# One pass over sixteen chunks, or over ten groups of one or two chunks

## The chip, the core and the metric

The kernel runs on one core of a Trainium2 chip. Its five engines work at the same time, each through its own list of instructions in order: TensorE (PE in the rows; its weight loads are PEld), VectorE (DVE), ScalarE (ACT), GpSimd (POOL) and SyncE (SP), which issues most of the DMA transfers. They wait for one another through semaphores. The metric is the device time of one execution in microseconds; three executions were timed, and the median counts.

## What is computed

One layer on 2048 tokens of width 128, all in float32: retention attention (linear attention with a decay for each of 8 heads), a residual and a layer norm, then a gated feed-forward part of width 352 whose inputs and weights are rounded blockwise (16 values share a scale) to a four-bit grid, and again a residual and a layer norm.

```python
q, k = rope(x @ Wq), rope(x @ Wk)          # 8 heads of 16
v, g = x @ Wv, x @ Wg                      # 8 heads of 32, width 256
scores = einsum('bhqd,bhkd,hqk->bhqk', q * DQK ** (-0.5), k, decay)   # decay is 0 above the diagonal
o = einsum('bhqk,bhkd->bhqd', scores, v)
o = o * rsqrt(mean(o * o, axis=-1) + EPS) * g_norm_w
x = layernorm(x + (o * silu(g)) @ Wo)
# quant(a): per 16 values, scale = max|a| / 6, each value to the nearest of 0, .5, 1, 1.5, 2, 3, 4, 6 times the scale
h = silu(quant(x) @ quant(w_gate).T) * (quant(x) @ quant(w_up).T)
x = layernorm(x + quant(h) @ quant(w_down).T)
```

## The kernel before

The 2048 tokens are cut into 16 **chunks** of 128 rows, one row to a partition. Attention inside a chunk is a 128 by 128 score tile for each head; what comes from earlier chunks is carried in a small state `S`, updated once for each chunk. So chunks depend on one another through the state alone, and a chunk goes through some forty steps ("stages") on four engines:

- TensorE: `project_qk` and `project_vg`; `transpose_qk`; `scores` (four matmuls, a pair of heads each); `state_product`; `from_state` and `values`, which add into one output; `transpose_o`; `transpose_y`; `out_projection`; then for the feed-forward part `transpose_xq`, `gate`, `up`, `transpose_h`, `down`.
- ScalarE empties most of the results out of PSUM (`copy_scores` into `raw`, `copy_oT`, `squares`, `copy_hT`, `silu_of_gate` and others), does one step of each rounding (`magic_x`, `magic_h`) and the scaling of both layer norms (`ln1_norm`, `ln2_norm`).
- VectorE rotates (`rotate`, three instructions), masks one pair of heads, updates the state, takes the mean square (`mean_square`, tile `ms`), multiplies by the gate (`gated`), adds the residuals, takes the layer norms' statistics and does five of the six steps of each rounding on `x` (128 wide) and on `h` (352 wide).
- GpSimd adds the rotated halves (`rotate_add`), masks the other three pairs of heads (`mask_scores`, `raw` to `probs`), takes the powers to minus one half (`rms_rstd` on 8 values a row, `ln1_rstd`, `ln2_rstd`), multiplies (`gated_output`, tile `y`) and scales back the rounded values (`x_value`, `h_value`).

Each engine's list is written out by the same loop over steps `s`, in which `run(stage, ahead)` issues the stage for chunk `s + ahead`, if there is such a chunk:

```python
for s in range(FIRST, LAST):
    run = stage_runner(s)
    run(state_product, 0)
    run(values, 0)
    run(transpose_xq, -4)
```

So the lines' order and the numbers beside them are the schedule, and nothing else orders the work but semaphores. On TensorE `transpose_xq`, `gate` and `up` are 4 chunks behind `values`, `transpose_h` 7 and `down` 8; on ScalarE the last step, `ln2_norm`, is another 5 behind. Results of TensorE lie in eight PSUM banks of 512 values a row, which several stages share; before a stage writes, it waits until the last tile of that bank was read (`free_scores_bank` and its like). Most tiles in SBUF have two or three buffers, taken by `c % 2` or `c % D`. The four weights are rounded and transposed once, in the gaps of the first steps. SyncE loads `x`, its transpose and the rotation tables in four parts of 1, 2, 5 and 8 chunks, and stores each chunk when it is done.

## Time and profile before

| | |
|---|---|
| timed, median of 3 (lowest to highest) | 140.3 us (139.18 to 141.06) |
| the profiled execution | 140.22 us, of which its trace spans 137.5 us |
| busy: TensorE, VectorE, GpSimd, ScalarE | 121.0, 115.8, 102.9, 97.3 us |
| granted TensorE clock | 0.999 of full speed |
| read and written in HBM | 5.26 MB and 1.05 MB |

The profiled execution lies 0.1 us below the median of the timed ones, and 2.7 us of it lie outside the span. "Busy" counts the time in which an instruction of the engine is under way; instructions of one engine overlap at their ends, so the distance from start to start of two neighbours is shorter than the first one's length where nothing holds the second up. A row of a time view gives start, length, engine, line of the kernel and instruction, and in brackets how long the engine was idle before it and who ended that.

### The profile page before, as it was taken

The numbers are of one execution on the slowest core, as the hardware profiler recorded it, in microseconds if no ns is written. First come the engines' busy times: TensorE is split into PE (matmuls) and PEld (weight loads), VectorE is DVE, ScalarE is ACT, GpSimd is POOL, SyncE is SP. The second block draws the span as 40 slices with busy tenths as digits, with TensorE's granted clock in tenths as the row PEclk, the third lists the DMA queues.
The fourth block names the chain that finished last, engine by engine and source line by source line (L and its number), as shares of the span: only waits on it lengthen the run. The fifth ranks groups of instructions, "written<-read, shape, count | busy, mean of one in ns | idle before, by whom it ended". The sixth has DMA issues, their size and how long they took to land.

```text
span 137.5 us, 3532 instructions
## 1 busy us (share of the span) xinstructions
PE 121.0 (88%) x1224; PEld 77.9 (57%) x1224; DVE 115.8 (84%) x438; ACT 97.3 (71%) x279; POOL 102.9 (75%) x139
## 2 busy tenths in 40 slices
PE   4986897998999999999999999999999878778650
PEld 4833354465656657585858585857575654445440
DVE  1269876867789999999999999999999899999940
ACT  3063965769787887988888888888888666665562
POOL 4204869577797979988888888889899985955692
PEclk9999999999999999999999999999999999999999
DMA  3899980000000000000000000000000000000113
GB/s 112 253 255 232 415 262 7 2 5 2 0 5 0 0 7 0 0 7 0 0 0 5 0 2 5 0 2 5 0 0 24 0 19 19 19 21 19 38 51 104
DMA packets 6897, 6.53 MB, mean 47 GB/s; under 512 B 864, under 2 KB 6112, under 8 KB 6752
## 3 DMA queue, kind: packets, MB, share of 16 engines
q1 hardware_dynamic: 5856, 5.56, 13.5%
q10 hardware_dynamic: 1024, 0.76, 1.7%
q8 instruction: 9, 0.15, 0.4%
q14 instruction: 8, 0.07, 0.2%
HBM read 5.26 MB, written 1.05 MB: 46 GB/s over the span
## 4 chain that ended last, share of the span: by engine, by line
PE 65%; ACT 12%; DVE 8%; DMA 5%; POOL 4%; issue 3%; SPq 1%; POOLq 0%; DVEq 0%; ACTq 0%
PE ps L464 7%; PE ps L480 7%; PE ps L352 6%; PE ps L392 5%; PE ps L335 4%; PE ps L382 4%; PE ps L326 4%; PE ps L457 3%; PE ps L471 3%; PE ps L416 3%; ACT q_eo L511 3%; PE ps L417 3%; DMA wd_nat<-in_w_down 3%; PE ps L365 3%; PE ps L449 3%
## 5 line engine op out<-in xcount | busy, mean ns | idle before, releaser
L899 POOL TENSOR_TENSOR rstd_h<-ms,minus_half 128x8 f32<-128x8 f32 x16 | 26.3, 1644 | 7.9 <-DVE ms L753 7.3
L910 POOL TENSOR_TENSOR rstd<-veps,minus_half 128x1 f32<-128x1 f32 x32 | 18.2, 571 | 1.4 <-DVE veps L769 1.2
L894 POOL TENSOR_SCALAR_AFFINE_SELECT probs<-raw 128x768 f32<-128x768 f32 x16 | 13.8, 863 | 6.9 <-ACT raw L510 6.4
L890 POOL TENSOR_TENSOR qk<-rope_c,rope_s 128x256 f32<-128x256 f32 x16 | 12.2, 766 | 8.2 <-DVE rope_s L730 7.8
L923 POOL TENSOR_TENSOR hq<-h_grid,hs 128x352 f32<-128x352 f32 x16 | 15.0, 935 | 2.9 <-DVE h_grid L667 2.9
L335 PE MATMUL ps<-w_vg,xT_sb 128*128 128x512 f32 x32 | 16.9, 610 | 0.1
L480 PE MATMUL ps<-wd_T,hT 128*128 128x128 f32 x96 | 13.6, 278 | 2.7 <-ACT hT L510 2.7
L464 PE MATMUL ps<-wgu_T,xqT 128*128 128x352 f32 x32 | 13.7, 510 | 1.1 <-DVE r L784 1.1
L480 PEld LDWEIGHTS ps<-wd_T,hT 128*128 128x128 f32 x96 | 12.1, 193 | 3.5 <-DVE r L784 2.6
L510 ACT ACTIVATE raw<-ps 128x768 f32<-128x768 f32 x16 | 13.0, 811 | 0.8 <-PE ps L352 0.6
L510 ACT ACTIVATE hT<-ps 128x384 f32<-128x384 f32 x16 | 7.8, 491 | 7.6 <-PE ps L471 7.6
L511 ACT ACTIVATE q_eo<-ps,consts 128x128 f32<-128x128 f32 x32 | 9.9, 365 | 4.2 <-PE ps L344 4.2
L352 PEld LDWEIGHTS ps<-q_eo,kT 32*128 32x128 f32 x128 | 5.0, 183 | 13.7 <-ACT kT L511 13.7
L352 PE MATMUL ps<-q_eo,kT 32*128 32x256 f32 x128 | 11.4, 426 | 0.9 <-ACT kT L511 0.6
L457 PE MATMUL ps<-wgu_T,xqT 128*128 128x352 f32 x32 | 12.2, 464 | 0.0
L904 POOL TENSOR_TENSOR y<-gate_o,rstd_h 128x256 f32<-128x256 f32 x16 | 10.8, 674 | 1.3
L726 DVE TENSOR_TENSOR rope_c<-ps,tabs_sb 128x256 f32<-128x256 f32 x16 | 6.6, 414 | 5.7 <-PE ps L326 5.5
L510 ACT ACTIVATE oT<-ps 128x256 f32<-128x256 f32 x16 | 6.1, 383 | 7.1 <-PE ps L392 7.1
L392 PE MATMUL ps<-probs,v_sb 128*32 128x128 f32 x256 | 10.6, 274 | 0.2 <-POOL probs L894 0.2
L574 ACT ACTIVATE o_sq<-ps 128x256 f32<-128x256 f32 x16 | 6.1, 384 | 6.5 <-PE ps L401 6.5
L806 DVE TENSOR_TENSOR h_blocks<-ps,silu_h 128x352 f32<-128x352 f32 x16 | 8.3, 522 | 2.5 <-PE ps L464 2.4
L326 PE MATMUL ps<-w_qk,xT_sb 128*128 128x256 f32 x32 | 10.4, 409 | 0.0
(108 smaller groups left out, 353.6 us busy)
## 6 DMA issues: line engine op xcount, KB each, us to landing
tabs_sb<-rope_tables SPq DMA_DIRECT2D x1, 1024.0 KB, 11.2
out<-x SPq DMA_DIRECT2D x16, 64.0 KB, 1.5
tabs_sb<-rope_tables SPq DMA_DIRECT2D x1, 640.0 KB, 7.8
xT_sb<-x_transposed SPq DMA_DIRECT2D x1, 512.0 KB, 9.1
x_res<-x SPq DMA_DIRECT2D x1, 512.0 KB, 11.8
xT_sb<-x_transposed SPq DMA_DIRECT2D x1, 320.0 KB, 6.6
x_res<-x SPq DMA_DIRECT2D x1, 320.0 KB, 8.3
w_vg<-in_w_vg ACTq DMA_DIRECT2D x1, 256.0 KB, 3.4
```

Source lines behind the costliest of these rows:

```text
L326: mm(qk_ps, xT(c), w_qk[:], start=True, stop=True).then_inc(qk_pe, 1)
L335: mm(vg_ps, xT(c), w_vg[:], start=True, stop=True).then_inc(vg_pe, 1)
L352: last = mm(sc_ps(j), kT[rows, c % D, :], q_eo[rows, c % D, :, :].rearrange("p e q -> p (e q)"), start=True, stop=True)
L392: last = mm(oT_ps[32 * slot32:32 * slot32 + 32, n // 4, :], v_sb[:, c % D, n * DV:(n + 1) * DV], probs[:, c % 2, n, :], start=c == 0, stop ...
L457: mm(gate_ps, xqT[:, c % 2, :], wgu_T[:, 0:I], start=True, stop=True).then_inc(gate_pe, 1)
L464: mm(up_ps, xqT[:, c % 2, :], wgu_T[:, I:2 * I], start=True, stop=True).then_inc(up_pe, 1)
L480: last = mm(down_ps, hT[:, c % 2, t, :], wd_T[:, t, :], start=t == 0, stop=t == 2)
L510: copy = lambda o, i: nc.scalar.activation(o, i, ACT.Copy)
L511: scaled = lambda o, i, by: nc.scalar.activation(o, i, ACT.Identity, scale=by)
L899: gp.tensor_tensor(rstd_h[:, c, :], ms[:, c, :], minus_half[:], ALU.pow).then_inc(rms_p, 1)
L910: gp.tensor_tensor(rstd[n][:, c, :], veps[n][:, c, :], minus_half[:, 0:1], ALU.pow).then_inc(ln_p[n], 1)
L923: gp.tensor_tensor(hq[:, c % 2, 0:I].rearrange("p (n k) -> p n k", k=BLK), h_grid[:, c % 2, :].rearrange("p (n k) -> p n k", k=BLK), hs[:, ...
```

## The change

The 16 chunks are put into ten **groups**: one chunk, six times two, three times one. The loop of each engine now runs over groups. Three kinds of stages are told apart: `run` calls a stage once for a group, `run_first` and `run_second` for its first and its second chunk.

A stage of a whole group is one instruction on VectorE, ScalarE or GpSimd, on twice the data where the group is a pair; on TensorE it is as many matmuls as before, behind one wait and with one signal at their end. Single by chunk are: `project_vg`, `from_state`, `gate`, `up`, `transpose_h` and the evacuations behind them (a bank holds one chunk of these), `next_state`, `h_product`, and what takes a scale or bias for each row and chunk (`ln1_centre`, `ln1_norm`, `ln2_norm`, the statistics of the layer norms). The widths of a pair's instructions: 512 for the rotation, gate and mask tiles of 256, 1536 for the scores' copy and mask, 256 for `x`, 704 for `h`, 16 and 2 values for the powers.

With it go: other places in PSUM (`QK`, `YT` and `ATT` share bank 4, `QKT` lies in bank 0 with scores, the two chunks' `oT` take banks 0 and 1, 2 and 3); two buffers for a group's tiles, by `g % 2`, and one only of `raw` and `probs`; a state for each chunk; the first and second layer norm and the output share one tile `r`; the tables in HBM are laid out by group; the loads have 1, 2, 4 and 9 chunks; the output is stored by group, in 10 transfers instead of 16. The lines of all four loops stand in another order, with other numbers beside them: on TensorE `transpose_xq` and the first `gate` are 3 groups behind `values`, `transpose_h` 6 and `down` 7, on ScalarE `ln2_norm` is 5 to 6 behind that. TensorE and the other engines compute the same results; the matmuls' number and shapes are the same.

```diff
--- before.py
+++ after.py
 MB = 1
 EPS = 1e-5
 
+SIZES = [1, 2, 2, 2, 2, 2, 2, 1, 1, 1]
+NG = len(SIZES)
+FIRSTS = [sum(SIZES[:g]) for g in range(NG)]
+
...
-        sc_ps = lambda j: ps[:, j, 0:256]
-        oT_ps = ps[:, 0:2, 0:C]
-        o_ps = ps[:, 2, 0:VD]
-        yT_ps = ps[:, 3, 0:VD]
-        qk_ps = ps[:, 4, 0:256]
-        qkT_ps = ps[:, 4, 256:512]
-        vg_ps = ps[:, 5, :]
-        att_ps = ps[:, 5, 0:H]
-        gate_ps = ps[:, 6, 0:I]
-        xqT_ps = ps[:, 6, 384:512]
-        hT_ps = ps[:, 6, 0:384]
-        up_ps = ps[:, 7, 0:I]
-        down_ps = ps[:, 7, 384:512]
-        U_ps = ps[:, 7, 0:2 * DV]
+        QK, QKT, VG, STATE, O, YT, ATT, XQT, GATE, UP, HT, DOWN = 4, 0, 5, 7, 2, 4, 4, 6, 6, 7, 6, 7
+        oT_ps = lambda i, half: ps[:, 2 * i + half, 0:C]
+        gate_ps = ps[:, GATE, 0:I]
+        up_ps = ps[:, UP, 0:I]
+        hT_ps = ps[:, HT, 0:384]
...
-        GROUPS = ((0, 1), (1, 3), (3, 8), (8, NC))
-        group = lambda c: next(g for g, (a, b) in enumerate(GROUPS) if a <= c < b)
-
-        FIRST, LAST = -4, 29
+        ends = [FIRSTS[1], next(f for f in FIRSTS if f >= 3), next(f for f in FIRSTS if f >= 7), NC]
+        LOADS = list(zip([0] + ends, ends))
+        load_of = lambda c: next(k for k, (a, b) in enumerate(LOADS) if a <= c < b)
+
+        first, size = FIRSTS.__getitem__, SIZES.__getitem__
+        last_of = lambda g: first(g) + size(g)
+
+        where = lambda c: (group(c) % 2, c - first(group(c)))
+
+        FIRST, LAST = -26, -1
         def stage_runner(s):
 
+
             def run(stage, ahead):
-                if 0 <= s + ahead < NC:
+                if 0 <= s + ahead < NG:
                     stage(s + ahead)
-            return run
+
+            def run_first(stage, ahead):
+                if 0 <= s + ahead < NG:
+                    stage(first(s + ahead))
+
+            def run_second(stage, ahead):
+                if 0 <= s + ahead < NG and size(s + ahead) == 2:
+                    stage(first(s + ahead) + 1)
+            return run, run_first, run_second
...
-            for c in range(NC):
-                sp.wait_ge(x2_act, c + 1)
-                sp.dma_start(out[c * C:(c + 1) * C, :], x2[:, c, :]).then_inc(d_out, 16)
-            sp.wait_ge(d_out, 16 * NC)
+            for g in range(NG):
+                sp.wait_ge(x2_act, last_of(g))
+                sp.dma_start(out[first(g) * C:last_of(g) * C, :].rearrange("(c p) n -> p c n", p=C),
+                             r[:, first(g):last_of(g), :]).then_inc(d_out, 16)
+            sp.wait_ge(d_out, 16 * NG)
...
-            def project_qk(c):
+            def project_qk(g):
                 pe.wait_ge(d_wqk, 16)
-                pe.wait_ge(d_x[group(c)], 16)
-                free_qk_bank()
-                mm(qk_ps, xT(c), w_qk[:], start=True, stop=True).then_inc(qk_pe, 1)
-                fill(4, "qk")
-                if c == 0:
+                pe.wait_ge(d_x[load_of(first(g))], 16)
+                free(QK)
+                for i in range(size(g)):
+                    last = mm(ps[:, QK, i * 256:(i + 1) * 256], xT(first(g) + i), w_qk[:], start=True, stop=True)
+                last.then_inc(qk_pe, 1)
+                fill(QK, "qk")
...
+            def scores(g):
+                pe.wait_ge(qkT_act, 3 * (g + 1))
                 for j in range(NP):
-                    free_scores_bank(j)
-                    rows = slice(32 * j, 32 * j + 32)
-                    last = mm(sc_ps(j), kT[rows, c % D, :], q_eo[rows, c % D, :, :].rearrange("p e q -> p (e q)"),
-                              start=True, stop=True)
+                    free(j)
                     tile[j] = "sc"
+                for i in range(size(g)):
+                    for j in range(NP):
+                        rows = slice(32 * j, 32 * j + 32)
+                        last = mm(ps[:, j, i * 256:(i + 1) * 256], kT[rows, g % 2, i, :],
+                                  q_eo[rows, g % 2, i, :, :].rearrange("p e q -> p (e q)"), start=True, stop=True)
                 last.then_inc(sc_pe, 1)
                 filled["sc"] += 1
...
-            def state_product(c):
-                if c == NC - 1:
+            def state_product(g):
+                chunks = [c for c in range(first(g), last_of(g)) if c < NC - 1]
-                free_up_bank()
-                pe.wait_ge(qk_p, c + 1)
-                pe.wait_ge(vg_act, c + 1)
-                for j in range(NP):
-                    last = mm(U_ps[32 * j:32 * j + 32, :], qk[:, c % D, 128 + 32 * j:160 + 32 * j],
-                              v_sb[:, c % D, 64 * j:64 * j + 64], start=True, stop=True)
+                free(STATE)
+                pe.wait_ge(qk_p, g + 1)
+                pe.wait_ge(vg_act, chunks[-1] + 1)
+                for i in range(len(chunks)):
+                    for j in range(NP):
+                        last = mm(ps[32 * j:32 * j + 32, STATE, i * 2 * DV:(i + 1) * 2 * DV],
+                                  qk[:, g % 2, i, 128 + 32 * j:160 + 32 * j], v_sb[:, g % 2, i, 64 * j:64 * j + 64],
+                                  start=True, stop=True)
                 last.then_inc(U_pe, 1)
-                fill(7, "U")
+                tile[STATE] = "U"
+                filled["U"] += len(chunks)
...
             def from_state(c):
-                pe.wait_ge(qkT_act, 3 * (c + 1))
+                g, i = group(c), c - first(group(c))
+                pe.wait_ge(qkT_act, 3 * (g + 1))
                 pe.wait_ge(state_v, c)
-                free_scores_bank(0)
-                free_scores_bank(1)
-                tile[0] = tile[1] = "oT"
-                filled["oT"] += 1
+                for half in range(2):
+                    free(2 * i + half)
+                    tile[2 * i + half] = "oT"
+                if i == 0:
+                    filled["oT"] += 1
                 if c == 0:
                     return
...
-            def down(c):
+                fill(HT, "hT")
+
+            def down(g):
                 pe.wait_ge(wT_act, 3)
-                free_up_bank()
-                pe.wait_ge(hT_act, c + 1)
-                for t in range(3):
-                    last = mm(down_ps, hT[:, c % 2, t, :], wd_T[:, t, :], start=t == 0, stop=t == 2)
+                free(DOWN)
+                pe.wait_ge(hT_act, last_of(g))
+                for i in range(size(g)):
+                    for t in range(3):
+                        last = mm(ps[:, DOWN, i * H:(i + 1) * H], hT[:, g % 2, i, t, :], wd_T[:, t, :], start=t == 0,
+                                  stop=t == 2)
                 last.then_inc(down_pe, 1)
-                fill(7, "down")
...
-                run = stage_runner(s)
-                run(state_product, 0)
-                run(values, 0)
...
+                run, run_first, run_second = stage_runner(s)
+                run_second(gate, 20)
+                run_second(project_vg, 24)
+                run(scores, 24)
+                run_second(up, 20)
...
-            def copy_scores(c):
-                act.wait_ge(sc_pe, c + 1)
-                copy(raw[:, c % 2, :, :].rearrange("p (j e) q -> p j (e q)", e=2), ps[:, MB:4, 0:256]).then_inc(
-                    raw_act, 1)
-
-            def copy_oT(c):
-                act.wait_ge(o_pe, c + 1)
-                copy(oT[:, c % 2, :, :], oT_ps).then_inc(oT_act, 1)
-
-            def squares(c):
+                copy(v_sb[:, b, i, :], ps[:, VG, 0:VD])
+                nc.scalar.activation(silu_g[:, b, i * VD:(i + 1) * VD], ps[:, VG, VD:2 * VD], ACT.Silu).then_inc(vg_act, 1)
+
+            def copy_scores(g):
+                act.wait_ge(sc_pe, g + 1)
+                k = size(g) * 256
+                copy(raw[:, :, 0:k], ps[:, MB:4, 0:k]).then_inc(raw_act, 1)
...
             def ln2_norm(c):
 
-                act.wait_ge(ln_v[1]["sum"], c + 1)
-                act.wait_ge(ln_p[1], c + 1)
-                scaled(x2[:, c, :], r[1][:, c, :], rstd[1][:, c, :]).then_inc(x2_act, 1)
+                act.wait_ge(ln_v[1]["sum"], group(c) + 1)
+                act.wait_ge(ln_p[1], group(c) + 1)
+                scaled(r[:, c, :], r[:, c, :], rstd[1][:, c, :]).then_inc(x2_act, 1)
...
-            def mask_scores(c):
+                cos, sin = (tabs_sb[:, a + m * n * H:a + (m + 1) * n * H].rearrange("p (g f) -> p g f", f=16)
+                            for m in range(2))
+                src, dst = g16(ps[:, QK, 0:n * 256]), g16(rope_s[:, b, 0:n * 256])
+                vec.tensor_tensor(g16(rope_c[:, b, 0:n * 256]), src, cos.unsqueeze(2).to_broadcast([128, 8 * n, 2, 16]),
+                                  ALU.mult).then_inc(rope_v, 1)
+                vec.scalar_tensor_tensor(dst[:, :, 0, :], src[:, :, 1, :], -1.0, sin, ALU.mult, ALU.mult).then_inc(rope_v, 1)
+                vec.tensor_tensor(dst[:, :, 1, :], src[:, :, 0, :], sin, ALU.mult).then_inc(rope_v, 1)
...
-            def ln_eps(n, c):
-                dve.wait_ge(ln_v[n]["aggr"], c + 1)
-                vec.tensor_scalar(veps[n][:, c, :], mv[n][:, c, 1:2], EPS, None, ALU.add).then_inc(ln_v[n]["eps"], 1)
-
+            def ln_eps(n, g):
+                dve.wait_ge(ln_v[n]["aggr"], last_of(g))
+                chunks = slice(first(g), last_of(g))
+                vec.tensor_scalar(veps[n][:, chunks, 0], mv[n][:, chunks, 1], EPS, None, ALU.add).then_inc(
+                    ln_v[n]["eps"], 1)
+
...
-            def rms_rstd(c):
-                pool.wait_ge(ms_v, c + 1)
-                gp.tensor_tensor(rstd_h[:, c, :], ms[:, c, :], minus_half[:], ALU.pow).then_inc(rms_p, 1)
-
+            def rms_rstd(g):
+                pool.wait_ge(ms_v, g + 1)
+                a, n = first(g), size(g)
+                flat = lambda t: t[:, a:a + n, :].rearrange("p c h -> p (c h)")
+                gp.tensor_tensor(flat(rstd_h), flat(ms), minus_half[:, 0:n * NH], ALU.pow).then_inc(rms_p, 1)
+
```

**TensorE, near the start.** In the rows `qk` and `kT` are the rotated keys and queries, `q_eo` the scaled queries, `oT` the heads' outputs. Before, from the projection of chunk 1 on, which follows the scores of chunk 0:

```order
L326 MATMUL ps<-w_qk,xT_sb 128x256
L365 MATMUL ps<-v_sb,qk 32x64 x4
L392 MATMUL ps<-probs,v_sb 32x128 x8
L400 MATMUL ps<-ident,oT 128x128
L401 MATMUL ps<-ident,oT 128x128
L343 MATMUL ps<-ident,qk 128x128
L344 MATMUL ps<-ident,qk 128x128
L335 MATMUL ps<-w_vg,xT_sb 128x512
L352 MATMUL ps<-q_eo,kT 128x256 x4
L326 MATMUL ps<-w_qk,xT_sb 128x256
```

Now, from the projection of the first pair, chunks 1 and 2, on:

```order
L326 MATMUL ps<-w_qk,xT_sb 128x256 x2
L336 MATMUL ps<-w_vg,xT_sb 128x512
L374 MATMUL ps<-v_sb,qk 32x64 x4
L406 MATMUL ps<-probs,v_sb 32x128 x8
L415 MATMUL ps<-ident,oT 128x128 x2
L348 MATMUL ps<-ident,qk 128x128 x4
L336 MATMUL ps<-w_vg,xT_sb 128x512
L360 MATMUL ps<-q_eo,kT 128x256 x8
L326 MATMUL ps<-w_qk,xT_sb 128x256 x2
L336 MATMUL ps<-w_vg,xT_sb 128x512
```

The transposes and scores of chunks 1 and 2 stand together, and the projection of chunks 3 and 4 right behind them; before, chunk 2's scores stood one whole turn behind chunk 1's.

**TensorE, at the end** (`xq` and `hq` are the rounded inputs, `wgu_T` and `wd_T` the weights, `hT` the transposed hidden values). Before:

```order
L457 MATMUL ps<-wgu_T,xqT 128x352
L464 MATMUL ps<-wgu_T,xqT 128x352
L471 MATMUL ps<-ident,hq 128x128 x3
L480 MATMUL ps<-wd_T,hT 128x128 x3
L471 MATMUL ps<-ident,hq 128x128 x3
L480 MATMUL ps<-wd_T,hT 128x128 x3
L471 MATMUL ps<-ident,hq 128x128 x3
L480 MATMUL ps<-wd_T,hT 128x128 x3
L471 MATMUL ps<-ident,hq 128x128 x3
L480 MATMUL ps<-wd_T,hT 128x128 x3
```

Now:

```order
L496 MATMUL ps<-ident,hq 128x128 x6
L506 MATMUL ps<-wd_T,hT 128x128 x6
L470 MATMUL ps<-ident,xq 128x128
L480 MATMUL ps<-wgu_T,xqT 128x352
L488 MATMUL ps<-wgu_T,xqT 128x352
L496 MATMUL ps<-ident,hq 128x128 x3
L506 MATMUL ps<-wd_T,hT 128x128 x6
L496 MATMUL ps<-ident,hq 128x128 x3
L506 MATMUL ps<-wd_T,hT 128x128 x3
L496 MATMUL ps<-ident,hq 128x128 x3
L506 MATMUL ps<-wd_T,hT 128x128 x6
```

Behind the last `gate` and `up` stood the hidden transposes and `down` of the last chunks in turn, four times; now the transposes of the last three groups (single chunks) stand before the `down` of a pair, of a single chunk, and of the last two single chunks in a row.

**ScalarE, at the end** (`hT` as above; `x` before and `r` now is the output that `ln2_norm` scales). Before:

```order
L510 ACTIVATE hT<-ps 128x384
L528 ACTIVATE h_magic<-h_ratio 128x352
L511 ACTIVATE x<-r,rstd 128x128
L510 ACTIVATE hT<-ps 128x384
L511 ACTIVATE x<-r,rstd 128x128
L510 ACTIVATE hT<-ps 128x384
L511 ACTIVATE x<-r,rstd 128x128 x7
```

Now:

```order
L544 ACTIVATE r<-r,rstd 128x128
L543 ACTIVATE hT<-ps 128x384
L561 ACTIVATE h_magic<-h_ratio 128x352
L544 ACTIVATE r<-r,rstd 128x128
L543 ACTIVATE hT<-ps 128x384
L544 ACTIVATE r<-r,rstd 128x128 x2
L543 ACTIVATE hT<-ps 128x384
L544 ACTIVATE r<-r,rstd 128x128 x12
```

Behind the last copy of `hT` stand 12 output scalings, where 7 stood before.

## Rows read from the trace of the kernel before

**Rows 1.** The page's first lines: span, and busy time, share and instructions of each engine.

```profile
span 137.5 us, 3532 instructions
...
PE 121.0 (88%) x1224; PEld 77.9 (57%) x1224; DVE 115.8 (84%) x438; ACT 97.3 (71%) x279; POOL 102.9 (75%) x139
```

**Rows 2.** Stretches: length; busy (count) of PE, PEld, DVE, ACT, POOL; clock, DMA.

```profile
20.40:38.42 18.02, 16.45 (x201) 9.94 (x198) 13.55 (x47) 13.18 (x39) 13.42 (x17) 1.00 0.02 4
38.42:56.09 17.67, 17.49 (x202) 10.60 (x202) 16.43 (x64) 14.30 (x45) 15.11 (x20) 1.00 0.01 2
60.79:101.34 40.55, 40.55 (x459) 27.20 (x458) 38.73 (x156) 32.73 (x97) 35.14 (x44) 1.00 0.01 2
107.99:137.50 29.51, 18.99 (x104) 12.33 (x103) 24.20 (x97) 17.24 (x48) 19.56 (x29) 1.00 0.12 34
```

**Rows 3.** Chain in order of time: start, length, what; one chunk's turn.

```profile
60.79 0.67 PE ps L480 x6
61.46 0.59 PE ps L457 x2
62.06 0.86 PE ps L335 x2
62.91 0.64 PE ps L352 x8
...
64.35 0.33 PE ps L471 x3
64.68 0.43 PE ps L326 x2
65.33 0.38 PE ps L382 x16
65.96 0.44 PE ps L392 x16
```

**Rows 4.** VectorE in order of time: start, length, instruction.

```profile
69.83 0.52 DVE L658 SCALAR_TENSOR_TENSOR h_ratio<-h_blocks,hs 128x352 f32<-128x352 f32 x1
70.27 0.29 DVE L761 BATCH_NORM_STATS2 stats<-r 128x6 f32<-128x128 f32 x1
70.47 0.41 DVE L736 TENSOR_TENSOR probs<-ps,causal 128x256 f32<-128x256 f32 x1
```

**Rows 5.** GpSimd's groups: busy time, mean ns of one, idle before it.

```profile
L899 POOL TENSOR_TENSOR rstd_h<-ms,minus_half 128x8 f32<-128x8 f32 x16 | 26.3, 1644 | 7.9 <-DVE ms L753 7.3
...
L910 POOL TENSOR_TENSOR rstd<-veps,minus_half 128x1 f32<-128x1 f32 x32 | 18.2, 571 | 1.4 <-DVE veps L769 1.2
...
L923 POOL TENSOR_TENSOR hq<-h_grid,hs 128x352 f32<-128x352 f32 x16 | 15.0, 935 | 2.9 <-DVE h_grid L667 2.9
...
L904 POOL TENSOR_TENSOR y<-gate_o,rstd_h 128x256 f32<-128x256 f32 x16 | 10.8, 674 | 1.3
...
L894 POOL TENSOR_SCALAR_AFFINE_SELECT probs<-raw 128x768 f32<-128x768 f32 x16 | 13.8, 863 | 6.9 <-ACT raw L510 6.4
```

**Rows 6.** GpSimd in order of time, one chunk's loop from mask to mask.

```profile
21.90 0.86 POOL L894 TENSOR_SCALAR_AFFINE_SELECT probs<-raw 128x768 f32<-128x768 f32 x1
...
27.19 0.62 POOL L904 TENSOR_TENSOR y<-gate_o,rstd_h 128x256 f32<-128x256 f32 x1
...
27.76 0.86 POOL L894 TENSOR_SCALAR_AFFINE_SELECT probs<-raw 128x768 f32<-128x768 f32 x1
```

**Rows 7.** Chain in order of time: chunk 1's transposes, chunk 4's scores.

```profile
13.01 0.33 PE ps L343
...
32.45 0.71 PE ps L352 x8
```

**Rows 8.** ScalarE at the end: last hidden copy, three and then the last output.

```profile
131.74 0.49 ACT L510 ACTIVATE hT<-ps 128x384 f32<-128x384 f32 x1 [1.16 <-PE ps L471]
...
132.13 1.01 ACT L511 ACTIVATE x<-r,rstd 128x128 f32<-128x128 f32 x3
...
135.07 0.40 ACT L511 ACTIVATE x<-r,rstd 128x128 f32<-128x128 f32 x1 [0.27 <-POOL rstd L910]
```

767 lines of the change are left out of this document (413 added, 354 removed).

## The prediction

> **What bounds the kernel now.** The page's first lines show TensorE busy 88% and VectorE 84% of the span [rows 1]; the stretches tell where. From 60.79 to 101.34 six chunks pass in 40.55 us, 6.76 us each, TensorE without a break and VectorE at 38.73 of 40.55 [rows 2]: TensorE is the bound, VectorE is just under it. The chain there gives its prices [rows 3]: `down` 0.67, `gate` or `up` 0.59, `project_vg` 0.86, `scores` 0.64, three transposes 0.33 (0.11 each), `project_qk` 0.43, `from_state` 0.38, `values` 0.44. With seven more transposes, `out_projection` at 2 x 0.22 (`down` is three such) and about 0.14 for `state_product` a chunk is 6.28 us of work; 0.48 us are gaps where stages change. Attention is 4.0 of it, `transpose_xq`, `gate` and `up` 1.3, `transpose_h` and `down` 1.0.
>
> Before that, TensorE has less to do and the kernel is no faster for it: 18.02 us for three chunks, then 17.67 us for three [rows 2], 6.0 and 5.9 each. What closes there is a loop through GpSimd: mask, `values`, `copy_oT`, `transpose_o`, `squares`, mean square, power, `y`, and the next chunk's mask, 27.76 - 21.90 = 5.86 us [rows 6], in which the power alone is 1.64 [rows 5]. After 107.99, when the last chunk's mean square starts, 29.5 us remain; VectorE is busy for 24.20 of them, TensorE for 18.99 [rows 2]. So there are three regimes: a latency loop, TensorE, and an end where VectorE's queue and latencies decide.
>
> **What an instruction costs on VectorE.** `h_ratio`, 352 wide, lasts 0.52 us, but its follower starts 0.44 us after it; the 128-wide statistics lets its own follower start after 0.20 [rows 4]. So a value costs 0.24/224 = 1.07 ns and 0.06 to 0.07 us are fixed per instruction from start to start. Of 26 instructions for a chunk, 20 become one for a pair: 10 fewer for each chunk of a pair, 0.65 us of 6.3. With these prices, summed over the whole list in its new order, VectorE goes from 107.8 us to 100.3 (438 instructions [rows 1] to 305). The Trainium skill (VectorE: DVE Perf Modes, section "The TRN2 errata") states a measured fixed term of about 150 cycles for each instruction, exposed between instructions, and advises wide tiles. At 0.157 us each the 133 fewer would save 21 us, not 8; the lengths agree with it (0.52 less 352 values is 0.15), the start distances do not, and I go by these.
>
> **The fill.** Chunk 0 stays alone, so I keep its times, up to the next transposes at 13.0 [rows 7]; with two chunks they end at 13.6. Then, worked from rows and doubled widths: three scaled copies 1.4, scores of both chunks 1.3 (until 16.3), copy of 1536 scores 1.45, mask 1.55 (below 2 x 0.863 [rows 5], above 0.863), `values` 0.9, `out_projection` of chunk 0 0.44, transposes of `oT` and of the next keys 1.3 with waits, until 22.1. With the copies 1.4 more the scores of chunks 3 and 4 start at 23.5. Chunk 4's started at 32.45 [rows 7]: **9 us earlier**, since one passage of the chain now carries two chunks.
>
> For a pair the loop of 5.86 grows by its wider instructions: mask 0.69; the power on 16 values; `y` 0.57; and 1.6 to 1.8 for `values`, `out_projection`, transposes, squares and mean square. The power took 1.644 us on 8 values and 0.571 on one, 0.153 a value, so 2.87 on 16, 1.23 more; the ends are 1.64 (nothing more) and 3.29 (double). The loop is then 9.9 us a pair, 5.0 a chunk in place of 5.9. By it the mean square of group 2 is at 32.0 us, with five chunks done.
>
> **The middle.** Seven turns follow, until the last group's mean square. TensorE's work in each, from the stages that its list holds there: 10.7 (8.0 attention, 1.4 weights, 1.3 the first feed-forward chunk), 9.4, 10.6, 10.3, 8.6, 8.6, 6.9. VectorE's, by its list: 5.4, 7.3, 9.5, 9.7, 9.8, 9.2, 8.2. Stages change about as often in a turn of two chunks as in one before, so I add 0.5 to TensorE's; where VectorE is longer I add 0.3, its loss in a 6.76 us turn being 0.3. The longer of the two: 11.2, 9.9, 11.1, 10.8, 10.1, 9.5, 8.5, sum 71.1. The last mean square starts at 32.0 + 71.1 = 103.1 us, 4.9 earlier than 107.99. So of 9 us gained in the fill 4 are given back: the feed-forward part now runs 3 to 7 groups behind, up to 12 chunks where it was 8, so that attention is nearly over before the first `down`, and three turns of one chunk are bound by VectorE with a pair's rounding in them. Shorter gaps alone would give 0.24 a chunk; that is in the sum.
>
> **The end.** From the last mean square to the last `h_grid` VectorE's list has 21.1 us. I add 1.5 for waits: at 125.7 us. `h_value` 0.94 [rows 5], transposes 0.33, `copy_hT` 0.49 and three handovers: 2.2, so 127.9. From the last mean square to the end of that copy it was 24.2 before (107.99 to 131.74 + 0.49 [rows 8]), now 24.8. Behind the copy the last chunk's `down`, residual, statistics, power and scaling take until 135.07 + 0.40, 3.2 us. Now ScalarE has 12 scalings queued there instead of 7, 0.30 us from start to start ((1.01 - 0.40)/2 [rows 8]), 3.7 us: a new wait, 0.5 longer than the chain it covers. Ends 131.6, and 2.0 for the last transfer as before (137.5 - 135.47): span 133.6, and with 2.7 outside it **136.3 us**. The profiled execution, 140.22, stands 0.1 below the median, so this is also the median's forecast: 3% faster.
>
> At no price I set: the merged loads and stores (transfers are idle, 0.02 and less, in the first three stretches [rows 2]); the new sharing of banks 4 and 0, since `rotate` (1.3 us) and the copies end before the next writer is due, 1.5 us or more of TensorE's work later; one buffer for `raw` and `probs`, whose next writer needs `values` anyway. If that cover fails a turn grows by some 0.3.
>
> **Rivals.** (1) *The pair's loop does not open.* With the feed-forward part in the list TensorE needs 10.3 to 10.6 for a turn, and by the same prices the mask ends only 0.4 us before `values` wants it. VectorE's long rounding instructions (704 values, 0.80 us) stand ahead of `mean_square`, GpSimd's `h_value` of 704 (1.7 to 1.9) ahead of the power, and `ln1_norm`, which waits for a power behind the next mask, stands ahead of `copy_oT`. If these put 1.2 us into each of six turns, the kernel takes 136.3 + 7.2 = 143.5 us, slower. From 0.7 us a turn it is slower than before, from 1.1 by over 2%. Against it: each such delay has some slack in the list, and the power may be cheaper than linear. GpSimd's rows also say that VectorE slows it: `y` has a mean of 0.674 [rows 5], against 0.62 where VectorE has much less to do [rows 6]. The Trainium skill (SBUF — State Buffer, section "SBUF: two separate sides") says that a VectorE instruction with two SBUF inputs and a GpSimd one lock each other out for a whole instruction, and these get longer here: by that 0.8 us at a time, which is this rival; the rows show stretches of 0.1 us.
>
> (2) *TensorE alone bounds the middle, and the end is as lean as before.* If VectorE's fixed cost that goes is nearer to the 0.15 us of its durations than to 0.07, it drops below TensorE in every turn: 65.1 + 7 x 0.5 = 68.6 in place of 71.1. With the power at some 2.2 in the fill and at the end (1.2 less) and 1.2 less of VectorE's list behind the last mean square, 131.4 us. This is also what the skill's fixed term above would make of the time.
>
> (3) *The gain of the fill is spent at the end.* The last groups are single, and each waits for VectorE, GpSimd, TensorE and ScalarE in turn, with little else queued; before, ScalarE stood 1.16 before the last copy of `hT` alone [rows 8]. With 5 us of waits in place of 1.5 it is 139.8: no change. That the change doesn't merge what it says is excluded by the list.
>
> **Chances and range.** The forecast's case 0.42 (133.5 to 139), the fast one 0.28 (129 to 133.5), the spent gain 0.14 (138.5 to 141), the closed loop 0.16 (140 to 147). The power's bounds are worth -1.5 and +2 us, the gaps' (0.2 to 1.0 a turn) -2 and +3.5. From 130.5 to 142 some eight in ten are held. A measurement of this kernel tells some 2% from no change, 2.8 us: faster than 137.5 has 0.28, and 0.29 of the 0.42; same (137.5 to 143.1) 0.28; slower 0.15, rounded.
>
> **What would show it.** Right: scores 8 matmuls at a time, the second such block at about 23.5 us; the power on 16 values near 2.87; the last mean square near 103; TensorE at 0.9 and more from 32 to 84 us and under it after; VectorE over 0.95 from 74 to 115; ScalarE with a dozen scalings without a break at the end. Wrong: TensorE waiting in each turn before `values` or `transpose_y` for GpSimd (rival 1), a last mean square before 100 (rival 2), or VectorE idle for more than 3 us after 105 (rival 3). The weakest steps are the 0.5 for gaps, and that a turn costs the larger of two sums although each engine waits for the other inside it.

## The result and the profile after

The changed kernel takes 141.09 us (median of 20 executions, 140.41 to 141.90), the one before 139.94 (20 executions beside them, 139.04 to 142.23): **1.0091 times the time, 95% interval 1.0062 to 1.0120**. It is 0.9% slower, where 3% faster was forecast. The ratios leave out executions over 1.5% slower than the fastest of the same kernel. The profiled execution has a span of 139.2 us and a time of 141.9, so it is the slowest of the 20, 0.8 us above the median.

The page of the changed kernel begins so (busy time and share of the span by engine; TensorE's clock in 40 slices, in tenths of full speed):

```profile
span 139.2 us, 3261 instructions
PE 120.4 (87%) x1224; PEld 80.2 (58%) x1224; DVE 110.4 (79%) x317; ACT 90.6 (65%) x219; POOL 94.3 (68%) x91
PEclk9999999999999999999999999999999999999868
```

Against [rows 1] VectorE has 121 instructions fewer (the prediction counted 133) and is busy 5.4 us less, but TensorE's work is the same. The mean squares mark the groups, which are counted from 0 (VectorE in order of time, groups 2, 3 and 9):

```profile
32.31 0.70 DVE L810 TENSOR_REDUCE ms<-o_sq 128x16 f32<-128x528 f32 x1
44.07 0.70 DVE L810 TENSOR_REDUCE ms<-o_sq 128x16 f32<-128x528 f32 x1
...
106.64 0.43 DVE L810 TENSOR_REDUCE ms<-o_sq 128x8 f32<-128x264 f32 x1
```

Below, "interval" is the time between the mean squares of two groups, and "end" the time from the last one to the end of the span. Three stretches of the same kernel (from 32.31, group 2's mean square; busy time of PE, PEld, DVE, ACT, POOL; clock, DMA) show where each engine is the bound, to be read against [rows 2]:

```profile
32.31:77.47 45.16, 44.12 (x542) 29.00 (x540) 34.99 (x95) 34.70 (x81) 34.94 (x26) 1.00 0.01 1
77.47:106.64 29.17, 27.66 (x257) 17.95 (x256) 28.99 (x80) 21.35 (x57) 23.77 (x20) 1.00 0.01 3
106.64:139.20 32.56, 21.67 (x120) 15.41 (x118) 24.93 (x90) 16.70 (x45) 17.68 (x22) 0.93 0.12 32
```

First TensorE is full (all but 1.04 us) and VectorE idles for 10 us. Then VectorE is full. The end is 3.1 us longer than the 29.5 of [rows 2]. So VectorE has idle time in the first stretch, where TensorE is the bound, and almost none in the second, where it is the bound itself.

The fill came as forecast: the scores of chunks 3 and 4 start at 24.08 where [rows 7] have chunk 4's at 32.45, and the power on 16 values takes 2.91 us.

```profile
24.08 1.15 PE L360 MATMUL ps<-q_eo,kT 32*128 32x256 f32 x16 [0.82 <-DVE gate_o L816]
```

But it isn't work done earlier. By 34 us TensorE has been busy for 28.3 us in the kernel before and for 28.6 us in the changed one:

```profile
0.00:34.00 34.00, 28.29 (x273) 17.28 (x274) 22.68 (x73) 19.86 (x52) 19.21 (x30) 1.00 0.51 156
```

```profile
0.00:34.00 34.00, 28.62 (x320) 18.73 (x320) 23.22 (x58) 19.51 (x44) 18.79 (x24) 1.00 0.50 156
```

The scores of chunk 4 are 8.4 us earlier, and the feed-forward part, which the old order did in that time, is later.

### The profile page after: what moved, and what is told of

It reads as the page before. It is cut to its first block, busy times and chain, and to the rows that moved or that the text cites. A ratio compares the mean times of both kernels' runs of the same rounds, so it can differ in the third digit from the quotient of the medians.

```text
span 139.2 us, 3261 instructions
## 1 busy us (share of the span) xinstructions
PE 120.4 (87%) x1224; PEld 80.2 (58%) x1224; DVE 110.4 (79%) x317; ACT 90.6 (65%) x219; POOL 94.3 (68%) x91
## 3 DMA queue, kind: packets, MB, share of 16 engines
HBM read 5.26 MB, written 1.05 MB: 45 GB/s over the span
## 4 chain that ended last, share of the span: by engine, by line
PE 50%; DVE 33%; ACT 6%; issue 4%; POOL 3%; POOLq 0%; DVEq 0%; ACTq 0%
PE ps L336 7%; PE ps L360 5%; PE ps L326 5%; PE ps L506 4%; DVE h_ratio L710 4%; PE ps L406 4%; PE ps L480 4%; PE ps L488 3%; DVE h_plus L715 3%; DVE hs L702 3%; PE ps L395 3%; DVE h_grid L719 3%; PE ps L435 3%; DVE h_blocks L876 3%; PE ps L319 2%
## 5 line engine op out<-in xcount | busy, mean ns | idle before, releaser
L983 POOL TENSOR_TENSOR rstd_h<-ms,minus_half 128x16 f32<-128x16 f32 (+1 forms) x10 | 24.0, 2404 | 13.9 <-DVE ms L810 13.9
L996 POOL TENSOR_TENSOR rstd<-veps,minus_half 128x2 f32<-128x2 f32 (+1 forms) x20 | 14.1, 711 | 10.0 <-DVE veps L829 9.9
L1013 POOL TENSOR_TENSOR hq<-h_grid,hs 128x704 f32<-128x704 f32 (+1 forms) x10 | 14.7, 1468 | 4.2 <-DVE h_grid L719 4.2
L974 POOL TENSOR_SCALAR_AFFINE_SELECT probs<-raw 128x1536 f32<-128x1536 f32 (+1 forms) x10 | 13.2, 1316 | 4.5 <-ACT raw L543 4.4
L968 POOL TENSOR_TENSOR qk<-rope_c,rope_s 128x512 f32<-128x512 f32 (+1 forms) x10 | 12.8, 1282 | 4.3 <-DVE rope_s L783 4.3
L506 PE MATMUL ps<-wd_T,hT 128*128 128x128 f32 x96 | 13.8, 295 | 0.5 <-DVE r L848 0.4
L543 ACT ACTIVATE raw<-ps 128x1536 f32<-128x1536 f32 (+1 forms) x10 | 11.9, 1194 | 3.5 <-PE ps L360 3.5
L496 PE MATMUL ps<-ident,hq 128*128 128x128 f32 x48 | 8.5, 288 | 3.9 <-POOL hq L1013 2.0
L990 POOL TENSOR_TENSOR y<-gate_o,rstd_h 128x512 f32<-128x512 f32 (+1 forms) x10 | 9.8, 975 | 0.8
L561 ACT ACTIVATE h_magic<-h_ratio 128x704 bf16<-128x704 f32 (+1 forms) x12 | 8.0, 665 | 3.1 <-DVE h_ratio L710 3.1
L715 DVE SCALAR_TENSOR_TENSOR h_plus<-h_magic,h_ratio 128x704 f32<-128x704 bf16 (+1 forms) x12 | 9.7, 818 | 0.0
## 6 DMA issues: line engine op xcount, KB each, us to landing
tabs_sb<-rope_tables SPq DMA_DIRECT2D x1, 1152.0 KB, 10.3
```

The lines of the kernel that those rows point to most:

```text
L496: last = transpose(hT_ps[:, t * C:(t + 1) * C], hq[:, b, i, t * 128:(t + 1) * 128], ident[:])
L506: last = mm(ps[:, DOWN, i * H:(i + 1) * H], hT[:, g % 2, i, t, :], wd_T[:, t, :], start=t == 0, stop=t == 2)
L543: copy = lambda o, i: nc.scalar.activation(o, i, ACT.Copy)
L715: vec.scalar_tensor_tensor(plus, magic, MAGIC, ratio, ALU.max, ALU.add).then_inc(count["plus"], 1)
L974: gp.affine_select(out=probs[:, MB:, 0:n, :, :].rearrange("p j i e q -> p j (i e) q"), in_=raw[:, :, 0:n * 256].rearrange("p j (k q) -> p ...
L983: gp.tensor_tensor(flat(rstd_h), flat(ms), minus_half[:, 0:n * NH], ALU.pow).then_inc(rms_p, 1)
```

## The experiments

Ratios are to the kernel before, with the 95% interval; the changed kernel itself has 1.0091. The table has, for each kernel, the intervals from group 2's mean square on and the end, worked out from the starts of the mean squares in each trace (us). TensorE's granted clock from 131 to 136 us stands beside the five kernels whose ends are compared by it. The intervals can be compared to 0.1 us, the spans can't: the first mean square starts anywhere from 13.8 to 15.6 us in these profiled executions.

```
forecast                 11.2 9.9 11.1 10.8 10.1 9.5 8.5  end 30.5
changed kernel           11.8 10.2 11.6 11.6 10.3 10.1 8.8  end 32.6  clock 0.66
e1_bank7                 10.7 10.2 11.6 11.6 10.3 10.1 8.8  end 31.5  clock 1.00
e2_down_first            11.7 10.2 11.6 11.6 10.3 10.1 8.8  end 31.7  clock 0.85
e3_fill_matmuls          11.8 10.2 11.6 11.6 10.3 10.1 8.8  end 32.8  clock 1.00
e4_ratio_first           11.8 10.2 12.0 11.5 10.5 10.3 8.8  end 33.6  clock 0.66
n0_state_early           10.4 10.2 12.0 11.9 10.3 10.1 8.8  end 31.5
t1_no_state_read         10.3 10.3 11.3 11.2 10.2 10.1 8.6  end 31.1
t5_no_power              10.6  9.9 11.6 11.6 11.1 10.3 9.0  end 31.0
t6_no_power_no_state     10.3 10.1 11.3 11.2 11.1 10.3 8.8  end 31.8
t2_half_rounding         10.6 10.2 11.6 11.3  9.7  9.7 8.4  end 29.4
t3_rotate_on_vector      11.0 11.0 11.9 11.3 10.2 10.1 8.8  end 31.5
```

**e1_bank7**, one wait:

```
-                    pe.wait_ge(wT_act, 2 if filled["weights"] == 1 else 3)
+                    pe.wait_ge(wT_act, 2 if bank == UP or filled["weights"] == 1 else 3)
```

> The changed kernel (1.009 times the time of the kernel before) with one wait shortened: the first state product of the pair in turn 3 waited 1.04 us for the copy of the down weights (bank 6), though its own bank 7 needs only the copy of the gate and up weights. Theory A (this wait is on the path of the middle turns): turn 3 shrinks by 0.6 to 1.0 us, the last mean square starts at 105.6 to 106.0 instead of 106.64, ratio 1.002 to 1.005. Theory B (the turn is set by another chain, GpSimd's or VectorE's): nothing moves, 1.007 to 1.011.

Measured: **1.0007, 0.9976 to 1.0039**. Group 3's mean square came 11.76 us after group 2's in the changed kernel and 10.65 here, so the wait of 1.04 us counted in full. This is TensorE's row of the changed kernel there (start, length, what, the idle time before it and who ended it):

```profile
39.37 0.43 PE L374 MATMUL ps<-v_sb,qk 128*32 128x64 f32 x16 [1.04 <-ACT wd_T L543]
```

TensorE idles for 1.04 us while ScalarE is still to copy another bank's weights: theory A, at a ratio just below its range (the last mean square starts at 106.39, later than it said, because the whole fill of that execution starts 0.8 us later). The two ratios differ by 1.2 us, each known to 0.4 us. So this wait is as much as the changed kernel lost against the one before, within what can be measured. One thing isn't separated from it: the granted clock, as a mean over an execution, was 0.982 to 0.993 in the 20 executions of the changed kernel and 0.991 to 0.996 in the 11 compared here. The following kernels, but for e2 to e4 and m1, have the edit too, and are compared with 1.0007.

**e2_down_first**, TensorE's order from the group's turn -10 on, with the old call kept for the turns ahead of that:

```
+                if s >= -10:
+                    run(down, 17)
                 run_first(transpose_h, 18)
```

> The changed kernel with the down products of a group ahead of the hidden transposes of the next group in TensorE's order, for the last groups only. Theory A (the end is 2 us longer than forecast because down of group 8 stands behind transposes that wait for the last hq, and down of group 9 then waits for the residual of group 8): the span from the last mean square to the end is 1 to 2 us shorter than 32.6, ratio 0.996 to 1.002. Theory B (the end is set by the last hq and the products' length at the lower clock): under 0.4 us, 1.006 to 1.010.

**e3_fill_matmuls**, up to 7 at the end of a turn, 3 ahead of the last transposes:

```
+            def filler(n):
+                free(3)
+                for _ in range(n):
+                    mm(ps[:, 3, 0:C], ident[:], ident[:], start=True, stop=True)
```

> The changed kernel with extra 128-wide matmuls into a bank that nothing reads, in TensorE's idle time of the last six turns (results unchanged). Theory A (TensorE's granted clock falls in the last 14 us because it idles, and the last down products last 1.29 and 1.53 us instead of 0.67 and 0.91 for that): clock over 0.9 there, last products 0.7 to 0.9, 0.7 to 1.2 us less, ratio 1.001 to 1.005. Theory B (the clock falls anyway, or the extra matmuls delay others by as much): 1.008 to 1.015.

Measured: e2 1.0096 (1.0055 to 1.0137), e3 1.0142 (1.0091 to 1.0193), theory B's ranges for both. The order of the products is worth nothing in the time, though e2's profiled end is 0.8 us shorter than the changed kernel's, at a higher clock. In e3 the clock stayed at 1.00 and the last two `down` took 0.83 and 0.94 us, its last mean square was no earlier against the first, and its end was 0.2 longer: the extra matmuls cost what they bring. That TensorE's clock is lower at the end of some executions is seen in the chain's last `down` products, of the changed kernel first, then of e1_bank7:

```profile
131.70 1.29 PE ps L506 x6
133.36 1.53 PE ps L506 x6
```

```profile
131.27 0.68 PE ps L506 x6
132.32 0.95 PE ps L506 x6
```

1.2 us between the two pairs, and the ends differ by 1.1. Both programs have the same instructions there; what differs is the wait some 90 us before, and whether it has to do with the clock at the end isn't shown. The changed kernel's 20 times don't follow its mean clock: the two executions at 0.988 took 140.4 us, the two at 0.993 took 141.6.

**e4_ratio_first**: `run(h_ratio_, 20)` moved ahead of `run(h_grid_, 19)` in VectorE's order.

> The changed kernel with VectorE's h_ratio (704 values) ahead of h_grid of the group before, so that it runs at another time than GpSimd's addition of the rotated parts, beside which it lasted 1.41 instead of 0.88 us in three turns. Theory A (such meetings stretch instructions and the turns with them): h_ratio near 0.88 in all turns, the turns 7 to 9 shorter by 0.3 to 0.5 each, ratio 0.999 to 1.005. Theory B (a meeting only moves to the next wide instruction, h_grid, 0.82 alone, and GpSimd waits as before): h_grid 1.2 to 1.4, turns unchanged, 1.007 to 1.012.

Measured: 1.0213 (1.0167 to 1.0259). Theory B, and worse than its range: the intervals together are 0.7 us longer than the changed kernel's and the end 1.0. VectorE's rows of the changed kernel, then of this one:

```profile
84.35 0.83 DVE L719 SCALAR_TENSOR_TENSOR h_grid<-h_magic,h_plus 128x704 f32<-128x704 bf16 x1
85.09 1.41 DVE L710 SCALAR_TENSOR_TENSOR h_ratio<-h_blocks,hs 128x704 f32<-128x704 f32 x1
```

```profile
85.26 0.89 DVE L710 SCALAR_TENSOR_TENSOR h_ratio<-h_blocks,hs 128x704 f32<-128x704 f32 x1
86.07 1.42 DVE L719 SCALAR_TENSOR_TENSOR h_grid<-h_magic,h_plus 128x704 f32<-128x704 bf16 x1
```

The stretch (0.53 us there, 0.6 here) stays and hits whichever comes second, beside GpSimd's addition; `h_grid`, for which GpSimd waits, now starts 7.8 us after the mean square instead of 6.9 and lasts longer.

**The sizes of the groups.** With e1's edit, `SIZES` is [1]*16; [1, 2, 2, 2] + [1]*9; and [1, 2, 2, 2, 2, 2] + [1]*5, with more turns in the loop.

> The changed kernel with the shortened wait of bank 7 (e1_bank7, 1.0007), and sixteen groups of one chunk: the new order of stages and no merged instruction. Theory A (merging is worth nothing by itself in the middle, since TensorE takes as long for a pair as for two, and its gain in the fill is spent by the longer distance to the feed-forward part): 0.99 to 1.01. Theory B (merging saves VectorE's fixed 0.06 to 0.15 us in some 130 instructions and GpSimd's, and most of that counts): 1.03 to 1.07.

> As h1_all_single, in groups of one, three pairs, nine single ones: pairs only where the latency loop of the fill decides. Theory A (pairs gain in the fill, and the lag of the feed-forward part that they make, counted in groups, costs at the end): better than e1_bank7, 0.97 to 0.99. Theory B (the end doesn't depend on the groups' size, VectorE's total does): worse than e1_bank7, 1.01 to 1.03.

> As h1_all_single, in groups of one, five pairs, five single ones. Theory A: between h2_three_pairs and e1_bank7, 0.985 to 1.000. Theory B: 1.002 to 1.012, between e1_bank7 and the kernel with more single groups.

Measured: 1.1557 (1.1496 to 1.1618), 1.0939 (1.0841 to 1.1038), 1.0353 (1.0290 to 1.0417). Theory A fails on all three, and theory B, right in sign, put the loss at less than half: in the new order merging is worth 22 us (162.10 against 140.05). The chain of h1 over one turn of one chunk (start, length, what) shows why:

```profile
82.89 0.28 ACT oT L543
...
83.21 0.44 PE ps L415 x2
83.65 0.61 PE ps L480 x2
...
84.28 0.46 ACT silu_h L632
84.74 0.26 ACT q_eo L544
...
85.57 0.71 PE ps L360 x8
...
88.83 0.28 DVE S L805
...
89.70 0.98 POOL rstd L996
...
90.76 0.40 ACT x_blocks L544
91.16 0.28 ACT oT L543
```

It comes back to its start after 8.27 us: `copy_oT`, transposes, SiLU and the scaled queries, scores, TensorE's list up to the state product, VectorE's first state update, `amax` of `h` (tile `hs`) and `eps`, GpSimd's power for the first normalisation, and `ln1_norm`, which stands ahead of `copy_oT` on ScalarE. The order before took 6.76 us a chunk [rows 2]. So the new order alone loses, and merging wins that back: two chunks in 10.2 to 11.6 us.

Now the other way: later pairs need the second state update ahead of the residual on VectorE.

```
                 run_first(next_state, 24)
+                run_second(next_state, 24)
```

> e1_bank7 (1.0007, 11.6 us in turns 4 and 5, span end 31.5 behind the last mean square) with VectorE's second state update of a pair right behind the first, which frees bank 7 earlier; it is also what later pairs need. Theory A (TensorE's own work bounds the middle): no change, 0.998 to 1.003. Theory B (the order on VectorE holds TensorE back there): 0.5 to 2 us less, 0.985 to 0.997.

> As n0_state_early, in nine groups: one, seven pairs, one. h3_five_pairs (eleven groups) was 1.0353, e1_bank7 (ten) 1.0007. Theory A (a turn costs what the pair's rounding in it costs, also where its attention is for one chunk, so that each group fewer saves): 3 to 5 us less than n0, 0.965 to 0.98. Theory B (pairs at the end lengthen the last chain, each of its steps having two chunks, by as much as a turn saves): 0.995 to 1.02.

> As n1_pairs_to_end, in eight pairs, also the first and the last. Theory A: one turn less again, but the first chain has two chunks, some 0.6 to 2 us: 0.95 to 0.98. Theory B (the first chain and the last chain with pairs cost more than a turn): worse than n1, 1.00 to 1.03.

Measured: n0 1.0075 (1.0034 to 1.0116), n1 1.0152 (1.0107 to 1.0197), n2 1.0325 (1.0267 to 1.0383). n0 costs 1 us, where 0 or a gain was expected: the two intervals of 11.6 are 0.35 and 0.32 us longer, and an earlier one 0.2 shorter. It is the loop of h1. VectorE's second state update, some 0.3 us, now stands ahead of `eps`. So GpSimd idles for 1.16 us before the first normalisation's power, where it was 0.84 in e1_bank7, and TensorE idles before the transposes behind `copy_oT`, where it never did in those two turns:

```profile
74.62 0.70 POOL L996 TENSOR_TENSOR rstd<-veps,minus_half 128x2 f32<-128x2 f32 x1 [1.16 <-DVE veps L829]
76.36 0.66 PE L415 MATMUL ps<-ident,oT 128*128 128x128 f32 x4 [0.20 <-ACT oT L543]
```

n1 saves a turn, its last mean square being 7.0 us earlier than n0's, at 100.5, and its end is 40.0 instead of 31.5: theory B. So is n2, a little above its range. Ten groups are the best of the six splits, of which the last two also have n0's edit.

**What a turn hangs on.** From e1_bank7, the products with the state left out; GpSimd's power on the mean squares made a multiplication; both; and, in VectorE's two last rounding steps, half of the values:

```
-                if c == 0:
+                if c >= 0:
                     return
```

```
-                gp.tensor_tensor(flat(rstd_h), flat(ms), minus_half[:, 0:n * NH], ALU.pow).then_inc(rms_p, 1)
+                gp.tensor_tensor(flat(rstd_h), flat(ms), minus_half[:, 0:n * NH], ALU.mult).then_inc(rms_p, 1)
```

```
+            h_half = lambda buf, g: buf[:, g % 2, 0:size(g) * I // 2]
```

> e1_bank7 with TensorE's products of the queries with the state left out, 0.76 us of each pair's turn (the output lacks the part that comes from earlier chunks). Theory A (TensorE bounds turns 4 and 5, VectorE turns 7 to 9): the intervals between mean squares from group 4 to 6 shrink from 11.6 to 10.9, those from group 7 on don't, the last mean square starts 1.5 to 2.5 us earlier. Theory B (a loop through all engines bounds every turn alike): all intervals shrink by the same 0.3 to 0.8, or none does.

> e1_bank7 with GpSimd's power on the mean squares (2.91 us for a pair) replaced by a multiplication (so the normalisation of the heads is wrong): the loop mask, values, squares, power, y is 2.7 us shorter. Theory A (in the fill and up to turn 4 the loop decides, from turn 5 TensorE's work and the loop end about together): the intervals from group 0 on, 8.8, 9.6, 10.7, 10.2, lose 1.5 to 2.7 each until TensorE's work of 10 to 11 stops it; those of 11.6 lose 0.2 at most; 10.3, 10.1, 8.8 nothing. Theory B (the loop decides in no turn after the fill): only the first two shrink.

> Both left out, the power and the products with the state (0.76 us of TensorE's work in a turn). Theory A (TensorE's work and the loop end together in turns 5 and 6, which is why t1 alone gave 0.3 to 0.4 of its 0.76): the intervals of 11.6 become 10.9. Theory B (TensorE alone, its durations overlapping): 11.2 as in t1_no_state_read. Turns 7 to 9 unchanged in both.

> e1_bank7 with VectorE's h_plus and h_grid on half of their values (the other half of the hidden values isn't rounded), 2 x 0.37 us less in the turn of a pair, 2 x 0.18 in that of one chunk. Theory A (VectorE bounds turns 7 to 9 and the end): the intervals 10.3, 10.1, 8.8 lose 0.7 to 0.8 each, the end 1.0 to 1.8 us, the earlier ones nothing. Theory B (the late turns hang on waits between engines): 0.2 to 0.4 each and under 0.8 in the end.

Measured once each: 137.82, 140.63, 138.38 and 137.19 us. t5 is the surprise: 2.7 us less in what the prediction took for the loop, and the first intervals go from 8.8 and 9.6 to 8.8 and 9.4, no other shrinks by more than 0.3, and one, in which VectorE is busy throughout, grows by 0.8. Neither theory. In t1 0.4 of the 0.76 come back in each of the two turns of 11.6, half of what theory A wanted, and in t6 the same: with the power gone too nothing more is gained. TensorE is no longer full there. It idles for 0.23 and 0.26 us in the two turns, in both kernels. In the first it waits for VectorE's rotation; what it waits for in the second a row of t1 shows:

```profile
74.17 0.66 PE L415 MATMUL ps<-ident,oT 128*128 128x128 f32 x4 [0.26 <-ACT oT L543]
```

It is the loop of h1, and ScalarE waits in it also in the changed kernel:

```profile
63.26 0.40 ACT L544 ACTIVATE x_blocks<-r_mean,rstd 128x128 f32<-128x128 f32 x1 [1.00 <-POOL rstd L996]
```

That loop holds one of the two `from_state` of a pair, 0.38 us, and so loses as much in t1. With n0, where the loop grows by 0.3 us and the turns by as much, this says that in these turns TensorE's work and the loop take the same time, to 0.1 us or so. Rival 1 feared this for another loop. t2 bears theory A out for the end (2.1 us less, from 2.6 less of VectorE's work) and half for the late turns (10.3, 10.1 and 8.8 become 9.7, 9.7 and 8.4, 1.4 us for 2.7 less of VectorE's work): VectorE is the bound there, and TensorE, busy in t2 for 27.1 of these 27.8 us, close behind.

**t3_rotate_on_vector**: GpSimd's `rotate_add` goes to the end of VectorE's `rotate`.

> e1_bank7 with the addition of the rotated parts on VectorE (some 0.6 us more of its work in a turn of a pair) instead of GpSimd (0.96 to 1.9 us less of its). Theory A (meetings with GpSimd cost VectorE about what they last, 0.5 us at h_ratio and 0.4 at x_grid in turns 7 to 9): h_ratio 0.88 there, VectorE's turns as long as before, and the fill 0.5 a turn shorter: 0.99 to 1.00. Theory B (each microsecond added to VectorE counts, since the meetings cost it nothing net): turns 7 to 9 0.5 longer, 1.008 to 1.02.

Measured: 1.0223 (1.0172 to 1.0274). The fill loses, intervals 8.8 and 9.6 becoming 9.5 and 10.8, as VectorE has the additions for pairs in it (1.13 and 1.80 us long there). The late turns don't: with 0.53 us more in VectorE's list they stay at 10.2, 10.1 and 8.8, and `h_ratio` is back at 0.88:

```profile
84.87 0.53 DVE L786 TENSOR_TENSOR qk<-rope_c,rope_s 128x256 f32<-128x256 f32 x1
87.55 0.88 DVE L710 SCALAR_TENSOR_TENSOR h_ratio<-h_blocks,hs 128x704 f32<-128x704 f32 x1
```

Theory A for the late turns (an addition on GpSimd costs VectorE what doing it itself would), B's sign in the total, just above its range.

**m1_port**, the price by itself.

> A kernel that leaves the layer out and writes zeros: VectorE and GpSimd instructions of this kernel's shapes alone and then side by side. Theory A (an exclusive lock between a VectorE instruction with two SBUF inputs and a GpSimd one): h_ratio's form of 704 values 0.88 alone and up to 1.4 to 1.8 beside GpSimd's additions of 512, the 352-wide one 0.52 and up to 1.0 to 1.4; the form with a PSUM input, and that with one input, unchanged; the additions 0.96 alone and longer in the first case only; the sum of both engines' work in the shared stretch about the sum of their lone times. Theory B (shared bandwidth): all forms stretched alike, in proportion to their length, about 1.3 to 1.6 times.

Its rows: busy time of VectorE and GpSimd in stretches where VectorE runs six of a form alone (`h_ratio`'s with 704 and 352 values, one with a PSUM input, one with a single SBUF input), then the first two beside GpSimd's additions of 512, `h_ratio`'s of 704 beside its power on 16, and the last two beside additions.

```profile
6.00:10.90 4.90, 4.89 (x6) 0.00 (x0) 1.00 0.00 0
10.90:13.67 2.77, 2.71 (x7) 0.00 (x0) 1.00 0.00 0
...
18.60:22.30 3.70, 3.68 (x6) 0.00 (x0) 1.00 0.00 0
22.30:25.10 2.80, 2.70 (x6) 0.00 (x0) 1.00 0.00 0
...
47.00:65.80 18.80, 18.80 (x11) 18.71 (x10) 1.00 0.00 0
67.40:82.20 14.80, 14.76 (x10) 14.77 (x10) 1.00 0.00 1
111.40:119.40 8.00, 8.00 (x10) 8.00 (x3) 1.00 0.00 0
144.40:152.80 8.40, 8.40 (x14) 8.40 (x7) 1.00 0.00 0
154.30:169.20 14.90, 14.90 (x11) 14.87 (x10) 1.00 0.00 0
```

Theory A, but for the one-input form: see the last section.

**The best of both**, e1 with e2, and with 11 extra matmuls at three places besides:

> e1_bank7 (1.0007) and e2_down_first together. Theory A (the order of the last down products costs something that a higher clock hides in e1_bank7's profile): 0.3 to 0.8 us less than e1_bank7, 0.995 to 0.999. Theory B (VectorE's queue sets the end, whatever the order of the products): 0.999 to 1.003, the end at 31.2 to 31.7.

> r1_wait_and_down with 11 extra matmuls into a bank that nothing reads, at three places of the last turns where TensorE waits (results unchanged). Theory A (the lower clock at the end costs 0.5 to 1 us in many executions, and these keep it up): 0.3 to 0.8 us less than r1, 0.993 to 0.998. Theory B (the clock isn't what the end waits for, or the matmuls delay others by as much): 0.999 to 1.008.

Measured: 1.0025 (0.9988 to 1.0062) and 0.9994 (0.9962 to 1.0026), with ends of 31.7 and 31.8 at a clock of 0.86 and 0.95. Theory B for both; that VectorE's queue sets the end is also what t2 showed. None of these kernels is measurably faster than the one before.

## Why the prediction was wrong

The forecast's span was 133.6 us, the profiled one is 139.2, 5.6 more: 0.3 in the fill, 3.2 in the middle, 2.1 at the end. By the medians it is 4.8, since the profiled execution is a slow one.

**The fill** was right to 0.3 us, but by luck, for a wrong reason. The prediction called the path through `y` and the power a loop; t5 took 2.7 us out of the power, and of that only 0.2 came back in the fill. Two other paths end together. One runs through the mask, `values`, `copy_oT`, the transposes and the scaled copies, the last of which ends at 23.69 us. The other, with which the chain of the profile ends this passage, is VectorE's queue, where the rounding of the weights stands ahead of `mean_square` and `gated` (their tiles are those of `h`); `gated` ends at 23.93, and the scores follow, from which on the chain is TensorE's own list to the end of the fill:

```profile
19.03 2.26 DVE h_plus L715 x2
21.29 0.86 DVE h_ratio L719
...
24.08 1.15 PE ps L360 x16
```

**The step that failed** is the sum over the middle, 71.1 us, measured 74.3, and in it the sentence "Stages change about as often in a turn of two chunks as in one before, so I add 0.5 to TensorE's". In the next three turns, where it was to apply, TensorE is busy without a break for 10.20, 11.63 and 11.57 us, against 9.9, 11.1 and 10.8 with the 0.5:

```profile
44.07:54.27 10.20, 10.20 (x132) 6.66 (x131) 8.27 (x25) 8.16 (x20) 7.99 (x6) 1.00 0.01 2
54.27:65.90 11.63, 11.63 (x139) 7.70 (x138) 10.09 (x27) 8.99 (x21) 9.46 (x7) 1.00 0.01 1
65.90:77.47 11.57, 11.57 (x137) 7.33 (x135) 10.52 (x27) 9.15 (x22) 9.72 (x7) 1.00 0.01 1
```

Of the 3.2:
- 1.1 us is a wait that the prediction did not have, the state product's for the down weights (e1_bank7). Without it that turn is 10.65, 0.5 under its forecast of 11.2.
- "Shorter gaps alone would give 0.24 a chunk": TensorE's list from one `up` to the next in a turn without `transpose_h` and `down` is 65.63 - 54.25 = 11.38 us in e1_bank7, 5.69 a chunk; before it was 6.76 less 0.33 and 0.67 [rows 3], 5.76. The gain is 0.07 a chunk. Against the 5.3 of work that the prediction had for these stages, 0.4 a chunk are gaps, so some 0.8 in a turn in place of 0.5. A pair's stages as a whole take nearly twice as long: what the scores save (1.07 us from start to start for 2 x 0.64) `values` (1.04 for 2 x 0.44) and `project_vg` (0.96 for 0.86, twice) lose. With the loop of h1 as long as TensorE's list in the second and third, the next three turns came out 0.3, 0.5 and 0.8 over.
- "Where VectorE is longer I add 0.3": the last three took 0.2, 0.6 and 0.3 more than that. In the first VectorE loses 0.53 us beside GpSimd (`h_ratio`, 1.41), in the second 0.53 and 0.42 (`h_ratio` and `x_grid`), in the third 0.42. The first turn and the second show `x_grid` without and with it:

```profile
80.78 0.41 DVE L719 SCALAR_TENSOR_TENSOR x_grid<-x_magic,x_plus 128x256 f32<-128x256 bf16 x1
...
90.55 0.83 DVE L719 SCALAR_TENSOR_TENSOR x_grid<-x_magic,x_plus 128x256 f32<-128x256 bf16 x1
```

**The end** was forecast at 30.5. In e1_bank7, where TensorE's clock is 1.00 from 131 to 136 us, it is 31.5 and goes as the forecast has it, up to the dozen scalings that set it on ScalarE:

```profile
131.31 0.49 ACT L543 ACTIVATE hT<-ps 128x384 f32<-128x384 f32 x1 [0.94 <-PE ps L496]
131.69 3.90 ACT L544 ACTIVATE r<-r,rstd 128x128 f32<-128x128 f32 x12
```

The last copy of `hT` ends 25.4 us after the mean square, where 24.8 was forecast: the last `h_grid` ends after 23.4, so the term of 21.1 + 1.5 for VectorE's list and waits was 0.8 short, and the 2.2 behind it took 2.05. The scalings take 3.9 (3.7), what follows them 2.3 (2.0). In the profiled execution of the changed kernel the end is another 1.1 longer, at the lower clock: its last two `down` hold two scalings back until 136.31.

**Rivals.** Rival 1's mechanism, the closed loop with `ln1_norm` ahead of `copy_oT`, is there, as long as TensorE's work and so of little cost by itself; its power on the mean squares was not in it. The 141.1 measured lie inside the range of 130.5 to 142, near its upper end, in rival 1's stretch and 0.1 above rival 3's, and in what the prediction called "same" (137.5 to 143.1), with a chance of 0.28. Rival 3's 139.8 is nearest, but its waits at the end aren't what made it: VectorE idles for 1.2 us between the last mean square and the last `h_grid`, not for 5. Rival 2 is excluded by the late turns, where VectorE is busy for 28.99 of 29.17 us. The forecast's own accounting, that of 9 us gained in the fill only 4 would be given back later, is what was most wrong: 1.4 us are left when the last mean square starts (106.64 against 107.99), and the end takes them and 1.7 more.

What stays open: how much of the 1.2 us between the changed kernel and e1_bank7 is the clock's, and why the two kernels' clocks differ at the end.

## What to carry to other kernels

When chunks are merged, count the engine's busy time up to a point, not how far the first stage has got: here the first stage was 8.4 us ahead with 0.3 us more of TensorE's work done. Merging pays where fixed costs or a latency loop bind, and the last groups then pay for the longer distance between the stages. After a change of order, look at each wait once more: one that names more than it needs was, within the margin, the difference between slower and equal. An instruction moved to GpSimd to relieve VectorE may cost VectorE its whole length.

## What the runs showed of the hardware

In m1_port `h_ratio`'s form takes 0.82 us from start to start alone with 704 values and 0.45 with 352 (4.90/6, 2.71/6). Beside additions of 512 on GpSimd the two engines take turns, one instruction each: 10 additions with 10 of the 704-wide in 18.7 us, with 10 of the 352-wide in 14.8. VectorE so loses 1.05 and 1.03 us per addition, whatever its own width; four additions alone take 4.92, 1.23 each:

```profile
25.18 4.92 POOL L163 TENSOR_TENSOR p_out<-p_a,p_b 128x512 f32<-128x512 f32 x4 [23.02 <-DVE wide L128]
```

The form with a PSUM input isn't touched (14 in 8.4 us, 0.60, as the 0.61 alone), nor does GpSimd's power touch `h_ratio`: 10 of the 704-wide take 8.0 us beside three powers, 0.80 each. The one-input form of 704 values goes from 0.45 to 1.49. Alone, 0.82 and 0.45 us make 1.05 ns a value and 0.08 us fixed from start to start, near the prediction's 1.07 ns and 0.06 to 0.07 us.

The Trainium skill (SBUF — State Buffer, section "SBUF: two separate sides") calls the port pair that VectorE and GpSimd share an exclusive lock held for a whole instruction, taken by VectorE's instructions with two SBUF inputs and by those in a two-port mode. The rows beside the additions agree, the one-input form's too if it ran in such a mode, which no row shows. The row beside the power does not: the power also has two SBUF inputs and lasts 2.9 us, and holds nobody up. Where they differ, the measurement decides. The prediction weighed this rule against stretches of 0.1 us in the old trace and set it aside; in the changed kernel `h_ratio` shows 0.53. The old trace had a longer one too: `x_ratio`, 0.26 us in the stretch that the prediction read, takes 0.62 twice in the fill, the second time beside GpSimd's addition (35.40 to 36.12):

```profile
35.65 0.62 DVE L658 SCALAR_TENSOR_TENSOR x_ratio<-x_blocks,xs 128x128 f32<-128x128 f32 x1
```

TensorE was busy 3.86 of 6.00 us from 125 to 131 in the changed kernel's profiled execution and 3.85 in e1_bank7's, with the same instructions. From 131 to 136 its clock was 0.66 of the full 2.4 GHz on average in the one, part of the time at 1.2 GHz, and 1.00 in the other. What makes the difference no row here shows; between these two executions the end differs by 1.1 us.
